# Moving one image's statistics and two pairs of group sums in a four-step chain of convolutions and an MLP

## The reference

```python
def _gn(v, G=4, eps=1e-05):
    B_, C_, H_, W_ = v.shape
    g = v.reshape(B_, G, C_ // G, H_, W_)
    m = jnp.mean(g, axis=(2, 3, 4), keepdims=True)
    s = jnp.var(g, axis=(2, 3, 4), keepdims=True)
    return ((g - m) / jnp.sqrt(s + eps)).reshape(v.shape)
...
x = x + _L0_conv_ref(_gn(x), L0_conv_weight, L0_conv_bias)   # 3x3, 8 -> 8
x = x + _L1_conv_ref(_gn(x), L1_conv_weight, L1_conv_bias)   # 3x3, 8 -> 8
x = x + _L2_conv_ref(_gn(x), L2_conv_w1, L2_conv_b1, L2_conv_w2, L2_conv_b2)  # 8 experts, 256 -> 1024 -> 256, exact gelu
x = x + _L3_conv_ref(_gn(x), L3_conv_weight, L3_conv_bias)   # 3x3, 8 -> 8
return x
```

## Time and profile before

| | us |
|---|---|
| median of three runs | 553.23 |
| lowest and highest | 550.0, 555.2 |
| profiled execution | 551.68 |
| its span | 549.9 |
| TensorE busy (matmuls) | 516.6, 94% |
| VectorE busy | 368.3, 67% |
| ScalarE busy | 296.4, 54% |
| GpSimd busy | 166.9, 30% |

### The profile page before, as it was taken

How to read it: one execution, slowest core, us unless ns; L and a number is a source line. 1 busy time by engine, 2 the same in 40 slices (tenths; PEclk the granted TensorE clock), 3 DMA queues, 4 the chain that set the end, 5 groups by cost and what they waited for, 6 DMA issues and landing times.

```text
span 549.9 us, 9211 instructions
## 1 busy us (share of the span) xinstructions
PE 516.6 (94%) x3391; PEld 258.1 (47%) x3391; DVE 368.3 (67%) x635; ACT 296.4 (54%) x366; POOL 166.9 (30%) x186
## 2 busy tenths in 40 slices
PE   1878999997899999999999999999999999999996
PEld 1433545554454444444444444444444445585542
DVE  4986999989866396096096096086084569989843
ACT  2889787735754454254254254254164492798360
POOL 3879678898370000000000000000000000188660
PEclk9997999999999999999999999999999999999999
DMA  8946455542110212022011021021023220026797
GB/s 316 383 127 155 119 130 134 134 147 104 50 77 1 77 78 76 1 76 74 2 76 66 10 76 60 17 76 52 24 76 132 98 77 0 4 57 176 234 325 277
DMA packets 13880, 57.41 MB, mean 104 GB/s; under 512 B 3084, under 2 KB 3212, under 8 KB 10764
## 3 DMA queue, kind: packets, MB, share of 16 engines
q1 hardware_dynamic: 12732, 53.80, 29.9%
q10 hardware_dynamic: 1116, 3.18, 1.7%
HBM read 30.03 MB, written 8.39 MB: 70 GB/s over the span
## 4 chain that ended last, share of the span: by engine, by line
PE 70%; DVE 17%; ACT 4%; DMA 2%; POOL 2%; issue 2%; SPq 1%; DVEq 0%; POOLq 0%; ACTq 0%
PE PS L1234 26%; PE PS L1208 25%; PE PS L1110 7%; PE PS L1103 6%; DVE ST L750 6%; DVE X L789 4%; DVE X L807 2%; PE PS L1165 2%; DMA HALO<-XN 2%; PE PS L1264 1%; SPq L274 1%; DVE XT L800 1%; ACT SCR L590 1%; PE PS L1181 1%; DVE HID L977 1%
## 5 line engine op out<-in xcount | busy, mean ns | idle before, releaser
L1208 PE MATMUL PS<-XT,W1S 128*128 (+1 forms) x768 | 169.5, 379 | 2.1 <-DVE XT L800 2.1
L1234 PE MATMUL PS<-HID,W2S 128*128 128x512 f16 x720 | 159.5, 379 | 0.0
L590 ACT ACTIVATE SCR<-PS,CONST 128x512 f32<-128x512 f32 x128 | 87.0, 685 | 62.1 <-DVE HID L930 27.5
L1208 PEld LDWEIGHTS PS<-XT,W1S 128*128 128x128 f16 x768 | 75.1, 98 | 89.9 <-issue 2.7
L1234 PEld LDWEIGHTS PS<-HID,W2S 128*128 128x128 f16 x720 | 70.4, 98 | 81.2
L432 POOL TENSOR_TENSOR XN<-SCR,XN 128x1024 f16<-128x1024 f32 (+1 forms) x60 | 99.0, 1679 | 11.4 <-ACT SCR L548 10.0
L814 DVE SCALAR_TENSOR_TENSOR W2S<-W2F,W2S 128x2048 f16<-128x2048 f32 x10 | 22.9, 2290 | 114.3 <-ACT W2S L586 114.3
L403 POOL MEMSET XN<- 128x128 f16 x6 | 2.8, 459 | 303.0 <-PE PS L1234 302.7
L750 DVE BATCH_NORM_STATS2 ST<-X 128x6 f32<-128x512 f32 x128 | 81.5, 680 | 7.4 <-DMA X<-x 6.3
L536 ACT ACTIVATE XN<-X,SC 128x1024 f16<-128x1024 f32 (+1 forms) x61 | 64.0, 1050 | 21.8 <-POOL SC L417 20.2
L789 DVE SCALAR_TENSOR_TENSOR X<-PS,X 128x512 f32<-128x512 f32 x96 | 59.9, 680 | 22.5 <-PE PS L1125 22.4
(11 more groups left out here) (55 smaller groups left out, 482.6 us busy)
## 6 DMA issues: line engine op xcount, KB each, us to landing
W1F<-w SPq DMA_DIRECT2D x10, 1024.0 KB, 4.8
W2F<-w SPq DMA_DIRECT2D x10, 1024.0 KB, 4.8
HALO<-XN SPq DMA_DIRECT2D x48, 129.9 KB
HALO<-XN SPq DMA_DIRECT2D x48, 121.8 KB
out<-X SPq DMA_DIRECT2D x11, 512.0 KB, 4.5
X<-x SPq DMA_DIRECT2D x2, 2048.0 KB, 18.6
HALO<-XN SPq DMA_DIRECT2D x40, 64.9 KB
HALO<-XN SPq DMA_DIRECT2D x40, 60.9 KB
```

Source lines behind the costliest of these rows:

```text
L590: act.activation(SCR[:, ft % 2, 0:CH], bank(ft % G_RING), ACT.Gelu, bias=BT[:, ds(e * FT + ft, 1)], scale=1.0 / (XS * WS)).then_inc(gelu_o ...
L1208: mm = pe.matmul(bank(ft % G_RING), W1S[:, w, h * NF + ft * P:h * NF + (ft + 1) * P], rhs, start=(n == 0), stop=(n == 3 * DH - 1))
L1234: mm = pe.matmul(bank(G2_BANK + h), W2S[:, w, ft * NW + h * P:ft * NW + (h + 1) * P], HID[slot][:, part, ft], start=(ft == 0 and part == 0 ...
```

## The change

On VectorE, all eight chunks of image 3 are read, and aggregated, in front of step 0's updates; before, five were read there and three after four of the updates. `deviation(2)` comes after the second of these chunks and `variance(2)` after the fifth; before, they came behind the fifth chunk and among the updates. Step 0 then joins the loop of the later steps, so that `deviation(3)` comes behind the first half's statistics and `variance(3)` behind the second half's updates.

On TensorE, `group_mean(2)` moves from the middle of the first tiles to the end of now 16 warm matmuls, four more warm matmuls follow, and `group_variance(2)` comes in front of the first tiles and no longer behind them. `group_mean(3)` moves from behind the second tiles to in front of them, and `group_variance(3)` from between the centres of step 1 to right behind the second tiles.

```diff
--- before.py
+++ after.py
@@ -61,7 +61,7 @@
           for n in range(4 * NCH)]
 HCH = CH // 2
 WARM_UP = 8
-WARM_TILES = 20
+WARM_TILES = 16
 
 THIRDS_BY_ACT = ((10, 0), (10, 1), (11, 0), (11, 1))
 RSTD_STEPS = 3
@@ -106,8 +106,6 @@
 
 
 POOL_LOW = (3, 5, 7, 9, 11, 13)
-
-LATE_STATS = 5
 
 EARLY_SUMS = 6
 
@@ -848,9 +846,13 @@
         for i in range(NCH):
             input_stats(2, i)
         aggregate(2)
-        for i in range(LATE_STATS):
+        for i in range(NCH):
             input_stats(3, i)
-        deviation(2)
+            if i == 1:
+                deviation(2)
+            if i == 4:
+                variance(2)
+        aggregate(3)
 
         def updates(g, i, n):
             for k in range(n):
@@ -860,20 +862,7 @@
             for k in range(n):
                 conv_stats(g, i + k)
 
-        updates(0, 0, 2)
-        variance(2)
-        updates(0, 2, 2)
-        for i in range(LATE_STATS, NCH):
-            input_stats(3, i)
-        aggregate(3)
-        stats(0, 0, QUAD)
-        updates(0, QUAD, QUAD)
-        deviation(3)
-        stats(0, QUAD, 2)
-        variance(3)
-        stats(0, QUAD + 2, 2)
-        aggregate(4)
-        for g in range(1, EARLY_SUMS):
+        for g in range(EARLY_SUMS):
             for i in range(0, NCH, QUAD):
                 updates(g, i, QUAD)
                 if i > 0:
@@ -1302,19 +1291,20 @@
         centre(0, 3)
         centre(0, 4)
         keep_warm(WARM_TILES)
-        tiles(0, 0, lambda: group_mean(2))
+        group_mean(2)
+        keep_warm(WARM_TILES // 4)
         group_variance(2)
+        tiles(0, 0)
         for i in range(QUAD + 1, NCH):
             centre(0, i)
+        group_mean(3)
         tiles(0, QUAD)
-        group_mean(3)
+        group_variance(3)
         for g in range(1, 8):
             before_step(g)
             for i in range(0, NCH, QUAD):
                 for k in range(QUAD):
                     centre(g, i + k)
-                    if (g, i, k) == (1, 0, 1):
-                        group_variance(3)
                     if i > 0 and k == 2 and g >= EARLY_SUMS:
                         group_variance(3 + g)
                 if i > 0 and g < EARLY_SUMS:
```

## The result

| | before | changed |
|---|---|---|
| median, us | 553.19 (11 runs) | 548.65 (11 runs) |
| lowest and highest | 550.0, 556.2 | 546.7, 553.3 |
| profiled execution | 551.68 | 553.26 |
| its span | 549.9 | 551.4 |

A forecast was written before the change was run, and what follows sets the result against it. TensorE mostly bounds the kernel, then VectorE. TensorE gets 6.2 us ahead in step 1, a held L765 loses 1 us, and 5.1 remain at variance(4): 553.23 - 5.1 = 548.1 us, range 545.0 to 551.5.

The forecast's parts named there:

- Bound and stall: TensorE bounds, then VectorE; in step 1 TensorE idles 1.15 and 1.73 us, then its clock is at 1.2 GHz.
- Image 2's sums: Mean and variance among warm matmuls: L765 ends at 29.5 in a GpSimd gap, first tiles stay at 31.07.
- rival (b): Image 2's L765 misses the gap at 29.44 and ends at 31.6: gain only 3.0 us, 550.2; chance 0.12.
- All of image 3 in front: Step 0: first updates at 33.5, second tiles at 36.4 for 36.62; up to here 0.2 us won.
- Step 1: Tiles at 42.7 for 47.22 and 48.2 for 54.37, at full clock; TensorE 6.2 us ahead.
- What is given back: Busy GpSimd holds L765 near 38.5 for about 1.0 us and near 50.0 for about 1.5; 1 us lost.
- rival (a): The L765s of images 3 and 4 are not held: 6.1 to 6.8 us gained, 546.8; chance 0.15.
- The sum without a hold: Without the rule of the shared SBUF port lock, the gain would be 6.2 us and not 5.1.
- The frozen advantage: Variance(4) at 53.9 for 59.04; the cycle of 11.40 stays, so 5.1 us last through later steps.
- The clock: TensorE's granted clock was to be 1.00 throughout 28 to 60 us.
- Rival (c): Clock falls before the first tiles, 28 to 32 us: costs 7.7 us or half; 557.9 or 554 with (b); chance 0.05.
- rival (d): Halo transfers come late for step 1's second half, needed at 48.2: up to 2 us lost, 551; chance 0.06.

## Why the prediction was right

- *Bound and stall.* Right. Putting image 3's chunks back brought both waits and the lower clock of step 1 back, and the median back to that of before. What the prediction didn't see is that it took the length of that fall from a single execution: with a fall as short as in the experiment, the 5.4 us at variance 4 would be 1.5 less, an estimate from 7.4 and 5.9 us for the same work.
- *Image 2's sums.* L763 of image 2 ended at 29.48, forecast 29.5; the first tiles started at 31.04 and 31.12, forecast 31.07. So rival (b) didn't come. The edit is worth 0.5 us at variance 4 and 0.9 from the next one on. The argument against (b) was weaker than it looks: the L765 at 20.43 got in behind a low part that no other followed, so only the one at 43.47 had slipped between two.
- *All of image 3 in front.* First updates 33.50, second tiles 36.37; forecast 33.5 and 36.4.
- *Step 1.* Tiles at 42.49 and 48.07, forecast 42.7 and 48.2, at full clock.
- *What is given back.* Two holds were forecast of 1.0 and 1.5 us and measured 1.01 and 1.56. That rules out rival (a). The Trainium skill, "SBUF — State Buffer", section "Who interferes with whom", says that a VectorE instruction with two SBUF inputs contends with a GpSimd one that reads SBUF. The trace agrees: with the same columns as scalars the holds vanish, 0.27 us against 1.56 with a second tensor. The sum without a hold, 6.2, would have been 0.8 too high at variance 4.
- *The frozen advantage.* 5.4 us at variance 4 for 5.1; the cycle of 11.4 stayed. But the advantage didn't stay frozen. At the end of the span 4.5 are left in this pair of profiles, and 4.5 in the medians. The trace places the missing 0.9. Some 0.6 go at the start of the MLP, where one `tensor_scalar` of VectorE (L913, L924 in the kernel before) takes 1.06 us at 134.29 for 0.43 at 139.61. And 0.4 go at 519.69, where tiles of the changed kernel wait 0.32 us for a halo transfer and those of before for none. What makes the first one longer wasn't tested. The two errors, 0.3 us too little at variance 4 and 0.9 lost behind it, partly cancel, so that the median came within 0.5 us of the forecast is in part luck.
- *The clock.* The text expected 1.00 from 28 to 60 us throughout. That failed in the very profile that came with the result. Rival (c) had the right place and the wrong price: it counted 7.7 us, or half of that if the clock recovers, and the fall took 1.5 us at variance 4, since the clock was back before the first tiles had ended. It was also tied to the wrong condition: the idle in front was 1.30 and 1.13 us in the two profiles of the changed kernel, with the lower clock in the first and not in the second, and 1.97 in the earlier trace rows without.
- *Halos*, rival (d): no tiles behind the first waited for a transfer before the MLP. Behind it, at 519.69, some did, for 0.32 us.

## What to carry to other kernels

When a stall is removed, ask which engine will now be busy at moments when it used to be idle, and what is issued against it there: here GpSimd, which now had work at those moments, made a 0.2 us instruction of VectorE take 1.0 and 1.6 us. What cured it here was the form of the instruction and not its place. And before one profile is read against another, compare the granted clock window by window: the first profile after this change was longer than the one before, though the change makes the kernel shorter. A stall that ends in a lower clock has no single price: in two executions with this stall the same work took TensorE 5.9 and 7.4 us.

## What the runs showed of the hardware

The granted clock of TensorE fell at places where it had waited (near 31, 134 and 537 us in the first profile of the changed kernel) in some executions of a kernel and not in others, with the same instructions. At the start of the MLP TensorE waits 1.76 us for VectorE in both profiles of the changed kernel; then the clock was 0.50 in the first and stayed at 1.00 in the second. An idle of 1.97 us in front of the first tiles left it at 1.00 in one execution, an idle of 1.30 was followed by 0.50 in another. The eleven runs of the changed kernel beside the result spread over 6.6 us, and the longest had the lowest mean clock, 0.990, the shortest the highest, 0.999. The mean clock isn't the whole spread: in the next set a run with 1.000 took 548.85 us and one with 0.995 took 547.89.

A VectorE `scalar_tensor_tensor` of 128x1 with two SBUF tensors took until the end of GpSimd's running low part, 1.99 us at most (at 94.30 in the kernel with the deviation two chunks earlier); the same arithmetic as `tensor_scalar` with both operands as scalar columns took 0.27 us in each of the cases read, 0.05 more than the unheld form's 0.22.
